# Moving the PSUM evictions of the Q and K projections from VectorE to ScalarE in an eight-core transformer layer

## The reference, cut to what matters

```python
# per core: x is one sequence, [2048, 2048]
q, k, v = heads(x @ Wq), heads(x @ Wk), heads(x @ Wv)      # 16 heads of 128
u = sigmoid(heads(x @ Wb)) * v
# scan over 32 chunks of 64 positions, per head
att   = where(mask, qq @ kk.T, 0)
o     = att @ uu + state applied to qq
state = state + outer products of uu and kk
x = layernorm(x + o @ Wo)
# feed-forward: activations quantised to 8 bit, weights replaced by their sign
xq = activation_quant(rms_norm(x))
p  = silu(xq @ sign(W_g).T) * (xq @ sign(W_u).T)
x  = layernorm(x + p @ sign(W_d).T)
```

## Time and profile before

| what | value |
|---|---|
| three timed runs, median (lowest to highest) | 7256.31 us (7065.99 to 7423.69) |
| the profiled execution, its own time | 7081.69 us |
| its span, first to last instruction, slowest core (core 1) | 7080.1 us |
| spans of the 8 cores | 6940.9 to 7080.1 us |
| mean granted TensorE clock of the cores | 0.821 to 0.826 of full speed |
| PE / DVE / ACT busy share of the span | 60% / 18% / 11% |

### The profile page before, as it was taken

The page is one execution under the profiler, slowest core; times in us unless marked ns, Lnnn a source line. Parts: engine busy times, 40 slices in busy tenths (PEclk is TensorE's granted clock), DMA queues, the critical chain, the costliest instruction groups (busy, mean ns, idle before and its releaser), DMA issues.

```text
span 7080.1 us, 56003 instructions; the slowest of 8 cores (6940.9 to 7080.1 us)
## 1 busy us (share of the span) xinstructions
PE 4281.6 (60%) x19440; PEld 1858.3 (26%) x19440; DVE 1307.3 (18%) x1766; ACT 751.7 (11%) x656; POOL 163.7 (2%) x313
## 2 busy tenths in 40 slices
PE   0052836383336443385579775798766797666997
PEld 0021412141113211142234222343222342222433
DVE  0000211021330215021001440013520025400101
ACT  0001211221112211101000001100011000011000
POOL 0000000010000100000000000000000000000000
PEclk9996767676767576677789987899888898888998
DMA  9978657775466743734333345243362334532433
GB/s 112 114 156 183 182 125 190 188 188 134 141 143 159 185 149 86 180 109 113 91 103 129 112 110 157 83 143 107 115 159 95 122 108 120 146 118 91 147 115 123
DMA packets 582380, 943.58 MB, mean 133 GB/s; under 512 B 150624, under 2 KB 306272, under 8 KB 574688
## 3 DMA queue, kind: packets, MB, share of 16 engines
q10 hardware_dynamic: 284928, 528.58, 22.8%
q0 software_dynamic: 45136, 184.57, 17.2%
q1 hardware_dynamic: 252048, 226.84, 11.4%
HBM read 906.23 MB, written 192.94 MB: 155 GB/s over the span
## 4 chain that ended last, share of the span: by engine, by line
DMA 31%; issue 17%; PE 15%; PEld 11%; another core or an unknown queue 6%; DVE 5%; ACT 4%; ACTq 4%; PEldq 4%; SPq 3%; DVEq 1%; POOL 0%; POOLq 0%
PEld pb L189 10%; PE pb L839 8%; DMA wdb<-swdT 7%; PE pb L189 5%; DMA ph<-swgT 4%; ACTq L152 4%; DMA ph3b<-wut 3%; ACT ph3b L262 3%; PEldq L180 3%; DMA swgT<-ph3b 3%; DMA ph3b<-wgt 3%; DMA ph3b<-wdt 3%; DMA swuT<-ph3b 2%; SPq L145 2%
## 5 line engine op out<-in xcount | busy, mean ns | idle before, releaser
L189 PE MATMUL pb<-ph3a,ph 128*128 128x512 bf16 x7680 | 1808.4, 389 | 660.3 <-DMA ph<-swgT 582.3
L189 PE MATMUL pb<-ph 128*128 128x512 bf16 x2400 | 601.5, 408 | 1668.3 <-DMA ph<-xt 429.4
L189 PEld LDWEIGHTS pb<-ph3a,ph 128*128 128x128 bf16 x7680 | 763.1, 100 | 1632.0 <-issue 779.5
L839 PE MATMUL pb<-wdb,ph 128*128 128x512 bf16 x4096 | 991.9, 394 | 305.2 <-DMA wdb<-swdT 275.0
L189 PEld LDWEIGHTS pb<-ph 128*128 128x128 bf16 x2400 | 245.7, 104 | 2003.7 <-issue 1762.8
L839 PEld LDWEIGHTS pb<-wdb,ph 128*128 128x128 bf16 x4096 | 383.6, 100 | 913.4 <-issue 616.5
L189 PE MATMUL pb<-ph,ph 128*128 128x512 bf16 x2400 | 560.4, 387 | 47.8 <-DVE ph3b L459 31.4
L794 DVE TENSOR_TENSOR ph<-ph,pb 128x512 bf16<-128x512 bf16 x256 | 176.0, 688 | 2236.7 <-PE pb L193 2147.8
L262 ACT ACTIVATE ph3b<-ph3b 128x2048 bf16<-128x2048 bf16 x192 | 366.6, 1909 | 1425.0 <-DMA ph3b<-wut 349.9
L189 PEld LDWEIGHTS pb<-ph,ph 128*128 128x128 bf16 x2400 | 237.0, 99 | 347.6 <-issue 79.6
L789 ACT ACTIVATE ph<-pb 128x512 bf16<-128x512 f32 x256 | 152.9, 597 | 1151.8 <-PE pb L193 1060.3
(11 more groups left out here) (69 smaller groups left out, 1546.1 us busy)
## 6 DMA issues: line engine op xcount, KB each, us to landing
ph<-swgT ACTq DMA_DIRECT2D x256, 256.0 KB, 8.4
ph<-swgT SPq DMA_DIRECT2D x256, 256.0 KB, 7.6
ph<-swuT SPq DMA_DIRECT2D x256, 256.0 KB, 8.2
ph<-swuT ACTq DMA_DIRECT2D x256, 256.0 KB, 8.6
wdb<-swdT SPq DMA_DIRECT2D x512, 128.0 KB, 2.3
wdb<-swdT ACTq DMA_DIRECT2D x512, 128.0 KB, 2.4
ph<-swq ACTq DMA_DIRECT2D x32, 1024.0 KB, 15.2
ph3b<-wgt POOLq DMA_DIRECT2D x64, 512.0 KB, 7.1
```

The source lines that it names most:

```text
L189: e.matmul(o, ll, rr, start=a, stop=False, skip_group_check=True))
L839: e.matmul(oo, ll, rr, start=a, stop=b, skip_group_check=True))
```

## The change

`q_evac` and `k_evac` evict with ACT in place of DVE. The copy is now in ACT's list, directly ahead of the issue of its own spill; it waits for what DVE's copy waited for (PE's group, and for Q the landing of the slot's last spill), and the event given back for `rot_free` is ACT's. Nothing else is changed: the same 64 copies for Q and 64 for K, the same DMAs, the same calls of `pump` and of `emit_quant_tb`, and PE's list is the same.

```diff
             def q_evac(tb, fg, bi, mm_ev):
                 j = (tb * 4 + fg) % 4
                 sl = ph3b[:, SS + j * 512:SS + (j + 1) * 512]
-                k.waits("vector", [mm_ev, stage_ev[j]])
-                v_ev = v_inc(lambda e, o=sl, i=pb[bi][:, :]:
-                             e.tensor_copy(o, i))
-                k.waits("scalar", [v_ev, prev_qtrr])
+                k.waits("scalar", [mm_ev, stage_ev[j]])
+                a_ev = a_inc(lambda e, o=sl, i=pb[bi][:, :]:
+                             e.copy(o, i))
+                k.waits("scalar", [a_ev, prev_qtrr])
                 stage_ev[j] = scq.batch(
                     [(sq[tb * 128:(tb + 1) * 128,
                          fg * 512:(fg + 1) * 512], sl)])
-                return v_ev
+                return a_ev
...
             def k_evac(tb, fg, bi, mm_ev):
                 sl = k_tok[:, tb * 2048 + fg * 512:tb * 2048 + (fg + 1) * 512]
-                k.waits("vector", [mm_ev, ktok_ufree])
-                v_ev = v_inc(lambda e, o=sl, i=pb[bi][:, :]:
-                             e.tensor_copy(o, i))
-                k.waits("scalar", [v_ev, prev_ktrr])
+                k.waits("scalar", [mm_ev, ktok_ufree])
+                a_ev = a_inc(lambda e, o=sl, i=pb[bi][:, :]:
+                             e.copy(o, i))
+                k.waits("scalar", [a_ev, prev_ktrr])
                 k_spill_evs.append(scq.batch(
                     [(sk[tb * 128:(tb + 1) * 128,
                          fg * 512:(fg + 1) * 512], sl)]))
-                return v_ev
+                return a_ev
```

## The result

| | before | after |
|---|---|---|
| timed runs, median (lowest to highest), 10 each | 7135.88 us (7042.85 to 7423.69) | 7357.11 us (7124.33 to 7577.63) |
| ratio after to before, 95% interval | | 1.0132 (1.0082 to 1.0181) |
| spans of the 8 cores in the profiled execution | 6940.9 to 7080.1 us | 7017.0 to 7122.8 us |
| first load of feed-forward weights issued, mean of the 8 cores | 3203.8 us | 3273.4 us |

The changed kernel is 1.3% slower, inside the 2% at which a difference is called one.

The account below looks back on a forecast made before the run. ACT's instruction list was taken to bound the attention half. K stages 98.0 us, Q 0 and table load -1.3 gave 96.7 us on 7081.7, so 7178 us, 1.4% above; range 7115 to 7270 us.

Parts of the forecast that it names:

- the term 7081.7: Base of the whole forecast: the profiled execution's 7081.7 us, 2.4% under the 7256 us median of three runs.
- The term of the change itself: Attention half: K stages cost 98.0 us, Q 0, table load -1.3 us; 96.7 us in all.
- B stage: ACT evicts 16 groups behind ten strips; its 56.0 us model the changed K stage, against 31.5 us before.
- The strips: Ten strips after K on ACT: no gain taken, though they could shrink by at most 8 and 7 us.
- the floor of 66: Low bound of the K cost over four tiles: 98 us less 4 x 8 us if strips after K shrink.
- K in tiles 2 and 3: Relief from DVE's quantisation valued at 0; PE's wait grows to about 177 us; each tile still costs 24.5 us.
- fourth rival: PE's two 108 us waits for K copies shrink by half, 6974 us, or vanish, 6866 us; chance 0.02.
- Q: Q stages on ACT: same loop of copy, issue and landing; 0 taken, bounds +1 and -1.5 us per tile.
- second rival: Weight loads and slow spill issues hold up Q and K copies mid-stage: 7226 us, or 7250; chance 0.13.
- Table load: ACT's first table load, before tile 0's first strip, moves to a Q copy where PE has a free bank: -1.3 us.
- third rival: Copies need their own table: 16 loads of 1.283 us around Q and K stages, 20.5 us, 7199 us; chance 0.05.
- first rival: Transfers are the bound and fill the longer K stage, so strips shrink as much: 7082 us; chance 0.10.

Follow-up runs that it names:

- K-only kernel: Only the K copies moved to ACT, Q copies left on DVE, against the kernel before: ratio 1.0085 (1.0046 to 1.0125).
- Q-only one: Only the Q copies moved to ACT, K copies left on DVE, against the kernel before: ratio 1.0050 (0.9997 to 1.0104).
- second profile of the change: The whole change, Q and K copies on ACT, run once more against the kernel before: ratio 1.0139 (1.0009 to 1.0269).

## Why the prediction was right or wrong

**What failed is the base of the sum.** I forecast 7178 us, 1.4% above a profiled execution of 7081.7, and a range to 7270; the measured median is 7357 us. The step that failed is the term 7081.7, taken with the sentence "I forecast on the scale of the undisturbed executions". The table before already had the profiled execution 2.4% under the median, and two of three runs above 7250; and the 16 us that I allowed between executions were drawn from two times, where ten runs of the kernel before go from 7043 to 7424 us. The term of the change itself was right: 97 us against a ratio of 1.0132 (0.0132 x 7066 = 93 us). The two medians are 221 us apart, so some 128 us of that are not the change but which executions came to stand in the middle of ten. Another median as base would not have made the sum sound: the 7136 us of the ten runs before gives 7233, 124 short, and the 7256 us of the table gives 7353, near the result by luck.

**The path was read rightly.** ACT's list is the path in the attention half, and DVE's K copies were off it. The copies moved onto it cost +101.3 us in the K stages over four tiles, against 98 forecast (25.3 us per tile, 24.5 forecast); the B stage was a true model of the K stage to come: 56.0 us forecast, 55.8 to 57.5 on the slowest core. Part of the stage's own history I did not see: what its 31 us before were. I read them as the price of 16 spills and two loads; the run with the spills on SyncE shows that the two weight loads alone hold ACT 26.0 us there. That did not touch the sum, since a measured stage stood on both sides.

**The strips.** I took no gain for them, with a floor of 8 us per tile. Behind K they gained little (299.4 to 292.5 us over four tiles; on the slowest core two of the four times ten last 69.5 and 69.6 us, below the 73 to 81 that I gave, and with them PE's waits in tiles 0 and 1, 70.9 and 68.2 us, lie below my 75 to 80). All strips of the half together got 26 us shorter; half of that, 12.9 us, is in the strips ahead of the K copies (267.1 to 254.2), which also shrink in the K-only kernel (255.7) and not in the Q-only one (269.9). Why is not shown, and the size is not sure: in the second profile of the change the strips of cores 0 to 3 are 12 us shorter than before, in the first 32. In the profile the net is +69.6 us, near the floor of 66; in the timed ratio it is 93 (58 to 128 us).

**K in tiles 2 and 3.** The relief of DVE behind the quantisation was worth nothing, as forecast: PE's longest wait went from 108.4 to 183.2 us, 177 forecast. The fourth rival, which had these waits shrink, is refuted.

**Q.** Forecast 0 within +1 and -1.5 us per tile: without the table load it is -1.2 us per tile in the changed kernel and -0.9 in the Q-only one. The second rival, that the weight loads in the middle hold the copies up, is refuted for K: the load takes 2.7 us there and the copies go on at PE's pace. For Q there is such a hold-up, but it was there before the change as well, which neither I nor the rival saw. The second copy behind the load goes into the slot of the first and waits 14 us until the spill of that one has landed. Tile 0 on core 5, DVE before and ACT after:

```profile
476.54 0.69 DVE L459 CAST ph3b<-pb 128x512 bf16<-128x512 f32 x1 [13.84 <-DMA sq<-ph3b]
478.01 0.59 ACT L459 CAST ph3b<-pb 128x512 bf16<-128x512 f32 x1 [13.95 <-DMA sq<-ph3b]
```

With the copies on ACT a Q stage lasts some 10 us longer than a K stage (66 and 56 us), and this is its longest wait; the change left it as it was.

**Table load.** One in place of one, now ahead of the first Q copy; no load at L489. The third rival is refuted, and with it stands what the Trainium skill has in ScalarE: Activation LUTs, section Table sets: the hidden batching unit, that copy is in every set: copies stand here between signs, sigmoids and square roots, and the number of loads is the same.

**The first rival** is wrong for this change. It fits the K stages of tiles 0 and 1 in the versions with strips among the copies, where the DMA share reached 1.01.

## What to carry to other kernels

When an eviction is moved to another engine, ask first what else stands in that engine's list ahead of it, and what the engine does while it waits for TensorE; its busy share (11% here) says nothing of either. The price was not 16 copies of 0.6 us but 16 groups of TensorE's time per tile in which the list held nothing else. Where a list alternates between long runs of two kinds of work that each wait for something else, put them among each other: that gave 4.4% here, more than three times what the choice of the engine took, and with it that choice made no difference that could be seen.

## What the runs showed of the hardware that I had not expected

ACT's next sign began only after the last of the eight was issued. The Trainium skill, page DMA: Bandwidth & Descriptors, section Issuing engines are not separate DMA queues, says that a DMA's start on the issuing engine is usually short beside the transfer, and that transfers of all engines share the same 16 DMA engines. The second half fits the run with SyncE's spills, where a tile took within 3 us the same from Q to B. The first held for the four issues, against a median of 11.3 us from issue to landing, and not for the eight. And ACT's copy of 128x512 from PSUM took 587 ns, 10 ns less than its sigmoid and 105 ns less than DVE's copy of a bank of the same size, none of which mattered to the time.
